# Half-wise turning of the first head's tiles, and two of four mask pieces marked on ScalarE: an attention layer with layer norm on one Trainium2 core

## The reference

```
N, HID, H = 2048, 256, 8             # x (2048, 256), adj (2048, 2048); n = 2048 tokens, d = 256
q = (x @ Wq).reshape(h, n, d); k = (x @ Wk).reshape(h, n, d); v = (x @ Wv).reshape(h, n, d)
a = einsum('hnd,hmd->hnm', q, k) * d**-0.5 + adj + adj
mask = adj == 0.0                     # about 255 of 256 elements
a = where(mask, -1000000.0, a); a = softmax(a); a = where(mask, 0.0, a)
out = einsum('hnm,hmd->hnd', a, v).transpose(1, 0, 2).reshape(n, h * d) @ Wout
return layernorm(x + out)
```

## Time and profile before

| | us |
|---|---|
| median of 3 runs | 1821.1 (1816.62 to 1823.1) |
| the profiled execution, device time | 1819.0 |
| its span, first to last instruction | 1817.3 |

### The profile page before, as it was taken

How to read it: one execution, slowest core, us unless ns; L and a number is a source line. 1 busy time by engine, 2 the same in 40 slices (tenths; PEclk the granted TensorE clock), 3 DMA queues, 4 the chain that set the end, 5 groups by cost and what they waited for, 6 DMA issues and landing times.

```text
span 1817.3 us, 29365 instructions
## 1 busy us (share of the span) xinstructions
PE 1791.5 (99%) x10272; PEld 1580.1 (87%) x10272; DVE 1097.2 (60%) x2318; ACT 852.5 (47%) x1411; POOL 983.7 (54%) x762
## 2 busy tenths in 40 slices
PE   8999899999999999999999999999999999999998
PEld 7987789888998889988898888988889888998886
DVE  6888855555555655555555555555555555546666
ACT  5654555444544445444454444544454444544433
POOL 7878864444644455455564445644455455544443
PEclk9999999999999999999999999999999999999999
DMA  7888875666646666566665666656665566655664
GB/s 252 252 254 270 265 222 155 197 184 189 190 142 200 193 181 197 143 197 189 189 185 157 199 186 180 184 157 198 197 188 158 165 198 200 183 156 174 183 171 133
DMA packets 186995, 345.97 MB, mean 190 GB/s; under 512 B 39392, under 2 KB 96736, under 8 KB 170464
## 3 DMA queue, kind: packets, MB, share of 16 engines
q10 hardware_dynamic: 92032, 200.59, 35.4%
q1 hardware_dynamic: 94816, 143.50, 28.7%
HBM read 190.84 MB, written 18.87 MB: 115 GB/s over the span
## 4 chain that ended last, share of the span: by engine, by line
PE 85%; SPq 5%; DVE 2%; DMA 2%; issue 1%; ACTq 0%; POOL 0%; ACT 0%; DVEq 0%
PE bank L409 33%; PE y_bank L425 22%; PE bank L374 18%; PE y_bank L433 12%; SPq L313 4%; DMA p_turned<-blocks 2%; DVE blocks L683 1%; ACTq L590 0%; POOL p_split L491 0%; DVE y_acc L770 0%; SPq L292 0%; DVE p_split L776 0%; PE bank L394 0%; ACT p_split L562 0%; DVE y_acc L705 0%
## 5 line engine op out<-in xcount | busy, mean ns | idle before, releaser
L491 POOL TENSOR_TENSOR p_split<-p_turned,p_split 128x512 fp32r<-128x512 f32 x510 | 650.1, 1304 | 543.3 <-ACT p_split L562 542.8
L409 PE MATMUL bank<-k_split,q_split 128*128 128x512 f32 x3072 | 788.2, 392 | 3.9 <-DVE small L660 3.9
L409 PEld LDWEIGHTS bank<-k_split,q_split 128*128 128x128 f32 x3072 | 556.5, 189 | 106.1 <-DVE small L660 5.2
L425 PE MATMUL y_bank<-v_split,p_split 128*128 128x512 f32 x2048 | 546.4, 389 | 1.3 <-ACT p_split L562 1.1
L660 DVE CUSTOM_DVE_ANT_0 t_p<-bank,m_sb 128x512 f32<-128x512 f32 x512 | 351.6, 687 | 212.1 <-PE bank L409 183.7
L425 PEld LDWEIGHTS y_bank<-v_split,p_split 128*128 128x128 f32 x2048 | 383.7, 188 | 83.1 <-ACT p_split L562 2.4
L553 ACT ACTIVATE t_p<-t_p,small 128x2048 f32<-128x2048 f32 x128 | 256.9, 2007 | 359.6 <-DVE small L672 351.0
L480 POOL TENSOR_TENSOR w_slot<-raw_w,w_slot 128x512 fp32r<-128x512 f32 x192 | 250.1, 1304 | 252.0 <-ACT w_slot L533 248.9
L562 ACT ACTIVATE p_split<-p_turned 128x512 fp32r<-128x512 f32 x512 | 288.0, 620 | 109.1 <-DMA p_turned<-blocks 105.4
L683 DVE STREAM_TRANSPOSE blocks<-t_p 128x2048 f32<-128x2048 f32 x128 | 295.9, 2312 | 65.9 <-ACT t_p L553 46.5
L374 PE MATMUL bank<-x_t,w_slot 128*128 128x256 f32 x2304 | 306.3, 285 | 7.7 <-issue 4.9
(11 more groups left out here) (44 smaller groups left out, 619.2 us busy)
## 6 DMA issues: line engine op xcount, KB each, us to landing
m_sb<-m_dram ACTq DMA_DIRECT2D x112, 1024.0 KB, 5.3
p_turned<-blocks SPq DMA_DIRECT2D x1532, 64.0 KB, 2.2
p_turned<-blocks ACTq DMA_DIRECT2D x516, 64.0 KB, 2.9
blocks<-in_adj_dram SPq DMA_DIRECT2D x64, 256.0 KB, 4.2
raw_w<-in_L_gnn_Wv_dram ACTq DMA_DIRECT2D x64, 256.0 KB, 3.4
m_dram<-m_sb SPq DMA_DIRECT2D x16, 1024.0 KB, 6.5
raw_w<-in_L_gnn_Wq_dram ACTq DMA_DIRECT2D x63, 256.0 KB, 3.4
raw_w<-in_L_gnn_Wk_dram ACTq DMA_DIRECT2D x61, 256.0 KB, 3.8
```

What stands on the lines that cost most here:

```text
L409: mm = nc.tensor.matmul(dst[:], q[:, a, k, f * P:(f + 1) * P], k_split[:, kk, k, b * BANK:(b + 1) * BANK], start=(i == 0), stop=(i == len( ...
L425: nc.tensor.matmul(y[:], p_split[tau % 2][:, HI, j * P:(j + 1) * P], v_split[:, j].rearrange("p s d -> p (s d)"), start=(j == 0), stop=False)
L491: nc.gpsimd.tensor_tensor(lo, p_turned[:, i * BANK:(i + 1) * BANK].rearrange("p (j b) -> p j b", b=QUAD), hi.bitcast(F32), ALU.subtract).t ...
```

## The change

1. **Halves.** In the first head (`in_halves`) the turn is two transposes of 128 x 1024, bands j = 0, 1 and then j = 2, 3. Each half waits for the exponential and for the shuffling of the same half of the tile before. The semaphores `shuffled` exist for each quarter and half, `turned` counts two a tile. SyncE issues the first half of all four quarters (8 transfers) after the first transpose, then j = 2 of all four (4 transfers) after the second; ScalarE's j = 3 are as before. The high part of a quarter waits for both halves.
2. **Marks on ScalarE.** For pieces 1 and 2 of tiles 1 to 15 VectorE no longer marks, and ScalarE makes Sign of the adjacency (into int8, 1 where it isn't zero) and, after a wait for that, Relu(-2^100 x sign + 2^100), which is 2^100 at the zeros and 0 elsewhere, with its row sum as the count. Both pieces are done one after the other at b = 1. GpSimd then subtracts this from the adjacency where it added before. VectorE scales the two counts back, and sums the counts at the head of the next iteration (`sum_counts`), where it was done after piece 3.
3. GpSimd fills a column with 2^100 as its first instruction, and ScalarE waits for it before its first weight load.

```
-    def shuffle(tau, i):
+    def shuffle(tau, i, columns):
         if i == 0:
-            sp.wait_ge(turned, tau + 1)
+            sp.wait_ge(turned, 2 * tau + 1 if in_halves(tau) and columns.start == 0 else 2 * tau + 2)
         if tau:
             sp.wait_ge(p_lo, 4 * (tau - 1) + i + 1)
-        for j in range(moved_by_sync(tau)):
+        for j in columns:
             sp.dma_start(p_turned[quad(j), i * BANK:(i + 1) * BANK],
-                         turned_place(tau)[quad(i), j * BANK:(j + 1) * BANK]).then_inc(shuffled[i], 16)
+                         turned_place(tau)[quad(i), j * BANK:(j + 1) * BANK]
+                         ).then_inc(shuffled[i][j // 2], 16)
...
                 load_y(t // 2)
-        for i in range(QUADS):
-            if tau:
-                shuffle(tau - 1, i)
-            if i == 1 and t == LAST_Q and h + 1 < H:
-                load_x(h + 1)
+        if tau and in_halves(tau - 1):
+            for i in range(QUADS):
+                shuffle(tau - 1, i, range(0, 2))
+                if i == 1 and t == LAST_Q and h + 1 < H:
+                    load_x(h + 1)
+            for i in range(QUADS):
+                shuffle(tau - 1, i, range(2, moved_by_sync(tau - 1)))
+        elif tau:
+            for i in range(QUADS):
+                shuffle(tau - 1, i, range(0, moved_by_sync(tau - 1)))
+                if i == 1 and t == LAST_Q and h + 1 < H:
+                    load_x(h + 1)
...
 def _(pool):
+    nc.gpsimd.memset(big[:], BIG).then_inc(big_filled, 1)
...
         pool.wait_ge(m_scaled, by_pool[a])
-        nc.gpsimd.tensor_tensor(m_piece(a), m_piece(a), adj_place[q].rearrange("p (r c) -> p c r", c=C),
-                                ALU.add).then_inc(m_by_pool, 1)
+        adj_piece = adj_place[q].rearrange("p (r c) -> p c r", c=C)
+        if marked_by_act(a):
+            nc.gpsimd.tensor_tensor(m_piece(a), adj_piece, m_piece(a), ALU.subtract).then_inc(m_by_pool, 1)
+        else:
+            nc.gpsimd.tensor_tensor(m_piece(a), m_piece(a), adj_piece, ALU.add).then_inc(m_by_pool, 1)
...
             act.wait_ge(y_done, tau - 1)
-        act.wait_ge(shuffled[i], 64 * (tau + 1))
+        act.wait_ge(shuffled[i][0], 32 * (tau + 1))
+        act.wait_ge(shuffled[i][1], 32 * (tau + 1))
...
             act.wait_ge(max_ready, t - 1)
-        act.wait_ge(marked, a + 1)
+        act.wait_ge(marked, nth_mark[a])
         nc.scalar.activation(m_piece(a), zero_mark[q % 2][:].rearrange("p (r c) -> p c r", c=C), ACT.Copy,
                              scale=-BIG).then_inc(m_scaled, 1)
 
+    def mark_zeros(t, q):
+        a = t * BANKS + q
+        if t >= 2:
+            act.wait_ge(m_stored[t % 2], 16 * (t // 2))
+            act.wait_ge(max_ready, t - 1)
+        act.wait_ge(adj_loaded[q], 16 * (t + 1))
+        if nth_signed[a] > 1:
+            act.wait_ge(m_scaled, by_pool[max(e for e in nth_signed if e < a)])
+            act.wait_ge(counted, t)
+        nc.scalar.activation(signs[:], adj_place[q], ACT.Sign).then_inc(signed, 1)
+        act.wait_ge(signed, nth_signed[a])
+        nc.scalar.activation(m_piece(a), signs[:].bitcast(U8).rearrange("p (r c) -> p c r", c=C), ACT.Relu,
+                             scale=-BIG, bias=big[:],
+                             accum_out=big_count[:, ACT_MARKS.index(q):ACT_MARKS.index(q) + 1]
+                             ).then_inc(m_scaled, 1)
+
     def shuffle(tau, i):
         if i == 0:
-            act.wait_ge(turned, tau + 1)
+            act.wait_ge(turned, 2 * tau + 2)
         if tau:
...
             act.dma_start(p_turned[quad(j), i * BANK:(i + 1) * BANK],
-                          turned_place(tau)[quad(i), j * BANK:(j + 1) * BANK]).then_inc(shuffled[i], 16)
+                          turned_place(tau)[quad(i), j * BANK:(j + 1) * BANK]
+                          ).then_inc(shuffled[i][j // 2], 16)
...
                 hi_p(tau - 2, 2 * b + 1)
-            if tau + 1 < TILES and b:
+            if tau + 1 < TILES and b == 1:
+                for q in ACT_MARKS:
+                    mark_zeros(t + 1, q)
+            if tau + 1 < TILES and b and b not in ACT_MARKS:
...
     def turn(tau):
-        if tau and turned_before(tau) is not None:
-            for i in range(QUADS):
-                dve.wait_ge(shuffled[i], 64 * (turned_before(tau) + 1))
-        elif tau:
+        if tau and turned_before(tau) is None:
             dve.wait_ge(m_by_pool, len(by_pool))
             dve.wait_ge(m_by_dve, len(by_dve))
-        dve.wait_ge(exp_done, tau + 1)
-        nc.vector.transpose(turned_place(tau)[:].rearrange("p (q j b) -> p j q b", q=QUADS, b=QUAD),
-                            t_p[:].rearrange("p (j q b) -> p j q b", q=QUADS, b=QUAD)
-                            ).then_inc(turned, 1)
+        for part in range(2) if in_halves(tau) else (None,):
+            if tau and turned_before(tau) is not None:
+                for i in range(QUADS):
+                    for half in (part,) if part is not None else range(2):
+                        dve.wait_ge(shuffled[i][half], 32 * (turned_before(tau) + 1))
+            dve.wait_ge(exp_done, tau + 1)
+            q = slice(0, QUADS) if part is None else slice(2 * part, 2 * part + 2)
+            nc.vector.transpose(
+                turned_place(tau)[:].rearrange("p (q j b) -> p j q b", q=QUADS, b=QUAD)[:, :, q],
+                t_p[:].rearrange("p (j q b) -> p j q b", q=QUADS, b=QUAD)[:, :, q]
+                ).then_inc(turned, 2 if part is None else 1)
...
 
+    def sum_counts(t):
+        if t:
+            dve.wait_ge(m_scaled, by_pool[t * BANKS + ACT_MARKS[-1]])
+            nc.vector.tensor_scalar(chunk_count[:, ACT_MARKS[0]:ACT_MARKS[-1] + 1], big_count[:],
+                                    1.0 / BIG, None, ALU.mult).then_inc(unscaled, 1)
+            dve.wait_ge(unscaled, t)
+        dve.wait_ge(marked, max(n for e, n in nth_mark.items() if e // BANKS == t))
+        nc.vector.tensor_reduce(count[:, t:t + 1], chunk_count, AX_X, ALU.add).then_inc(counted, 1)
+        dve.wait_ge(counted, t + 1)
+        nc.vector.tensor_scalar(no_mask[:, t:t + 1], count[:, t:t + 1], 0.0, NO_FLOOR,
+                                ALU.is_equal, ALU.mult).then_inc(floor_part, 1)
+        dve.wait_ge(floor_part, t + 1)
+        nc.vector.tensor_scalar(maxima[:, t, BANKS:BANKS + 1], no_mask[:, t:t + 1], FLOOR, None,
+                                ALU.add).then_inc(floors, 1)
+
     def build(t, q):
         a = t * BANKS + q
+        if marked_by_act(a):
+            return
...
                 dve.wait_ge(m_stored[t % 2], 16 * (t // 2))
-            dve.wait_ge(marked, a + 1)
+            dve.wait_ge(marked, nth_mark[a])
             nc.vector.scalar_tensor_tensor(
...
                 op0=ALU.mult, op1=ALU.add).then_inc(m_by_dve, 1)
-        if q == BANKS - 1:
-            dve.wait_ge(marked, a + 1)
-            nc.vector.tensor_reduce(count[:, t:t + 1], chunk_count, AX_X, ALU.add).then_inc(counted, 1)
-            dve.wait_ge(counted, t + 1)
-            nc.vector.tensor_scalar(no_mask[:, t:t + 1], count[:, t:t + 1], 0.0, NO_FLOOR,
-                                    ALU.is_equal, ALU.mult).then_inc(floor_part, 1)
-            dve.wait_ge(floor_part, t + 1)
-            nc.vector.tensor_scalar(maxima[:, t, BANKS:BANKS + 1], no_mask[:, t:t + 1], FLOOR, None,
-                                    ALU.add).then_inc(floors, 1)
+        if a == BANKS - 1:
+            sum_counts(t)
...
                 moments((tau - LAG - 1) % TILES)
+        if 1 <= tau < TILES:
+            sum_counts(tau)
         if tau + 1 < TILES:
             build(t + 1, 0)
         if 1 <= tau < ALL:
```

24 lines of the change are left out of this document (20 added, 4 removed).

## The result

| | before | after |
|---|---|---|
| median, 14 runs each on one chip, us | 1819.83 (1816.62 to 1823.41) | 1823.1 (1820.45 to 1826.31) |
| profiled execution, device time | 1819.0 | 1826.3 |
| its span | 1817.3 | 1824.6 |
| ScalarE busy | 852.5 | 878.1 |
| VectorE busy | 1097.2 | 1093.7 |

The ratio of after to before is 1.0017, 95% interval 1.0009 to 1.0024: the change costs about 3 us. That is within the 0.3% that counts as the same, but on the other side of the forecast (6.4 us faster), and it lies 0.1 us above the end of the range. The profiled execution of after is the highest of its 14. The same kernel, profiled again as e11, has a span of 1820.5 us, 3.2 above before, and is the nearer look where the size of the loss counts.

The account below looks back on a forecast made before the run. First head bound by the turn-transfer-landing loop, 13.0 us a tile, later heads by TensorE. To 12.1 + 0.3 = 12.4: 6.6 us over eleven steps, less 0.2 at the start, 1821.1 - 6.4 = 1814.7 us; range 1808.5 to 1823.

Parts of the forecast that it names:

- The queue turns into one without idle: 12.1 us a tile: SyncE's queue, first head: starting transfers sooner removes 0.9 us idle a tile, 13.0 to 12.1, with the same number of transfers.
- The prediction's loop: First head, tiles 3 to 14: VectorE's turn, SyncE's twelve transfers, landing, next turn; 13.0 us a tile, forecast 12.4.
- nothing is won: Rival, chance 0.20: transfer engines are the limit, a shorter queue only lengthens landings, second half-turn still waits; 1820 us.
- the 0.3 us for later landings: First-head transfers: landings 0.6 us later allowed, counted as 0.3 us a tile over the two kinds of tile.
- They need all pieces, so this costs little: ScalarE's high parts: they start after the exponential anyway, and the last piece lands as late as before; little cost.
- The scaling of the two counts comes in, 0.16 us: VectorE, each tile: one small added instruction, priced like the reduction over four numbers, 0.16 us.
- Start: 0.2 us: ScalarE's first weight load waits for GpSimd's fill, delaying TensorE's first projection; 0 to 0.4 us, 0.2 taken.
- Relu with its sum: ScalarE's marks: Relu reading a bias column and writing a row sum, taken at 0.87 us a piece.
- half a turn: VectorE, first head: one 128x1024 transpose, taken at 1.2 us, letting the first eight transfers start sooner.
- that rival: Table switches on ScalarE, chance 0.04: Sign outside the exponential's set, two table loads a tile; 17 us more, 1838 us.
- slower through ScalarE: Rival, chance 0.12: ScalarE's lump of marks waits for adjacency loads; at 13.6 us a tile, 1828 us.
- the ceiling of 10.4: TensorE's stops from 160 to 250 us: 9.5 us idle plus 7 x 0.135 hidden, the most the change can return.

Follow-up runs that it names:

- e11: The changed kernel (after) unaltered, profiled and measured again beside e12; ratio to before 1.0014, span 1820.5 us.
- the light kernels: Kernels storing and reading back only the first 512 of 2048 columns of each mask tile; ratios to before 0.9943 to 0.9960.
- e1: After with halved turn and transfers only; all marks back on VectorE, no fill at the start; ratio to before 1.0011.
- e12: After with the two counts scaled by two one-number instructions, the repeat run of e3; ratio to before 1.0010.
- e5: As e1, but SyncE issues its twelve transfers in the old order, quarter by quarter, after both half turns; ratio to before 1.0001.
- e2: After with turn and transfers undivided, so only the marks on ScalarE remain; ratio to before 1.0035.
- e9: Before with four small VectorE probe multiplications a tile from the third head on (1, 2, 3 numbers, 2 apart); one run, no ratio given.
- e4: After with turn and transfers undivided and the two counts scaled by one-number instructions; ratio to before 1.0007.
- e14: After undivided, ScalarE's marks only from tile 4 on, both counts scaled in one instruction; ratio to before 0.9997.
- e8: After undivided, ScalarE's marks only from tile 4 on, the two counts scaled one by one; ratio to before 0.9998.
- e6: Before with only the first 512 of 2048 columns of each mask tile stored and read back; ratio to before 0.9954.
- e16: The kernel of e6 (before with the light mask store) run again; ratio to before 0.9951.
- e7: e1 with only the first 512 of 2048 columns of each mask tile stored and read back; ratio to before 0.9943.
- e3: After with the two counts scaled by two one-number instructions instead of one instruction on both; ratio to before 1.0029.
- e13: e1 with halves only up to tile 10, turn and transfers undivided from tile 11 on; ratio to before 1.0001.

## Why the prediction was wrong

**"The queue turns into one without idle: 12.1 us a tile."** This is the step that failed. The idle time did go (8.1 to 2.9 us), and the first transfers start earlier. But the step took the length of the twelve issues as fixed, and that is not so: they took 8.0 us in the light kernels, 8.66 in before, 9.5 in after. That is 0.85 us more a tile, 7.7 in the nine tiles from 85 to 204 us, and 4.7 of it are the waits for GpSimd's low parts shown above. The chain that ended last passes there, after:

```profile
186.16 3.04 DMA p_turned<-blocks
...
189.31 0.64 ACT p_split L594
...
190.02 5.06 POOL p_split L519 x4
195.07 0.10 SPq L332
```

Before's chain goes from the landing to the next turn and back to SyncE's issues. This one goes from the landing over ScalarE's high part and GpSimd's four low parts to SyncE's issues, which wait for them, and the chains of e1, e11 and e12 do so too. The prediction's loop didn't have this way. It is not the only limit, though, since e5 has hardly any of these waits and a pace of 13.03. The pace stayed at 12.9 to 13.1 in every kernel with the full traffic, whichever engine had been relieved, and went to 12.1 to 12.4 in every kernel without the store's three quarters. The prediction's rival "nothing is won", at 0.20, has the outcome and half of the mechanism: the landings did get longer, but the second half of the turn waited for one in one tile of twelve in after (two in e1). In the sum, the 0.3 us for later landings is the mis-sized term: what was needed was 0.9 to 1.0.

**"They need all pieces, so this costs little."** This failed too, and what the waits show as cost of the halves comes from it: the late high parts, and the late low parts behind them. The premise was that the last piece lands as late as before. With all of j = 2 issued at the end, though, all four quarters become whole together and late, where they had become whole one after the other. ScalarE, which works in order, then waits: 2.3 us before, 7.1 with the old order (e5), 16.4 with the new (e1), 19.9 in after (where the marks add to it, see e2 and e4). After's TensorE in order of time, 202 to 210 us:

```profile
202.04 1.64 PE L436 MATMUL bank<-k_split,q_split 128*128 128x512 f32 x6
206.09 1.83 PE L452 MATMUL y_bank<-v_split,p_split 128*128 128x512 f32 x4 [2.41 <-ACT p_split L594]
207.72 2.58 PE L436 MATMUL bank<-k_split,q_split 128*128 128x512 f32 x6
```

What is queued behind the wait suffers too. ScalarE from 226 to 240 us, after:

```profile
228.41 0.62 ACT L564 ACTIVATE w_slot<-raw_w 128x512 fp32r<-128x512 f32 x1
...
233.64 0.63 ACT L594 ACTIVATE p_split<-p_turned 128x512 fp32r<-128x512 f32 x1 [4.61 <-DMA p_turned<-blocks]
...
235.17 0.62 ACT L564 ACTIVATE w_slot<-raw_w 128x512 fp32r<-128x512 f32 x1
```

The next head's weight (235.17) stands behind the high parts, and TensorE's chain of waits there has a hole:

```profile
234.43 3.73 issue
238.16 1.83 PE bank L401 x7
```

The prediction listed who waits for the exponential and left out who stands behind a late quarter.

**What the profiled runs lost, in sum.** The stretch from 205 to 250 us in e11, in e1, and in e9, whose first head is before's:

```profile
205.00:250.00 45.00, 39.26 (x226) 34.25 (x227) 32.03 (x69) 28.63 (x52) 34.38 (x27) 0.96 0.87 267
```
```profile
205.00:250.00 45.00, 42.14 (x238) 37.24 (x237) 31.67 (x76) 26.96 (x46) 35.69 (x27) 0.92 0.89 271
```
```profile
205.00:250.00 45.00, 39.83 (x231) 35.07 (x232) 31.17 (x73) 26.40 (x46) 33.40 (x25) 0.96 0.88 276
```

The second head's first scores come 8.2 us later in after than in before. TensorE's idle from 160 to 250 us accounts for 11.0 - 9.5 = 1.5, tile 3's later scores for 2.2, and the granted clock of 0.89 for 0.11 x 45 = 5.0 us of work at full speed: 8.7. For e11 it is -0.1, 2.0 and 0.04 x 45 = 1.8, together 3.7 of 4.2. For e1 the idle is 8.15, so -1.4, with 0.1 before 160 us; the start gives -0.5 and the clock 3.6: together 1.8 of 1.9. So in these executions TensorE's idle time was hardly longer than before, in e1 even shorter, and the lower clock behind the stops made up the rest. This is a term that the prediction doesn't have at all. It can't simply be charged to the change: e9, with the first head of before, has 0.96 there too, and its second head starts at 243.9 us where it starts at 241.6 in before's profile. Against e9, e11 is 1.9 us late at the second head and was 2.0 late at tile 3 already, and e1 is 0.4 early. So before's profile is a lucky one in this respect, and the part of the loss that stands in both comparisons is the late start of tile 3, 2 of about 3 us.

**"The scaling of the two counts comes in, 0.16 us."** Mis-sized by nine: 1.43 us. The form with more than one number in a partition waits for GpSimd's running instruction (e9). In the undivided kernel from tile 1 on it costs 5 us (e2 against e4), from tile 4 on nothing (e14), with halves nothing measurable (e12 against e11). The prediction priced it by a row of a reduction over four numbers, which doesn't wait. A rule of the Trainium skill spoke against that price and was not weighed: "SBUF — State Buffer", section "Who interferes with whom", says that a tensor_scalar whose operands meet the conditions can enter a mode that takes the port pair shared with GpSimd, that whichever comes second blocks for the whole instruction, and that a reduction never contends on this chip. The probes on two numbers agree, 90 of 90.

**"Start: 0.2 us."** The fill was what was looked at. What costs is the lump of marks: four ScalarE instructions and two sum reads stand in tile 0 ahead of the key's weights. ScalarE, 24 to 28 us, after:

```profile
24.49 0.63 ACT L625 ACTIVATE signs<-blocks 128x512 int8<-128x512 f32 x1
25.15 0.78 ACT L627 ACTIVATE m_sb<-signs,big 128x512 f32<-128x512 uint8 x1
...
26.41 0.62 ACT L564 ACTIVATE w_slot<-raw_w 128x512 fp32r<-128x512 f32 x1
```

and TensorE's stop behind them:

```profile
28.48 1.66 PE L401 MATMUL bank<-x_t,w_slot 128*128 128x256 f32 x12 [0.97 <-issue]
```

A second new stop, of 0.99 us, ends at 62.25 us, for VectorE (1.16 in e11). Tile 3 is 2.2 us late (2.0 in e11), and with no gain in the loop behind it that delay is never made up. Kernels that leave the first tiles alone (e8, e14) have neither the delay nor a loss.

**What came out as said.** Sign 0.63 us (0.65 taken), Relu with its sum 0.765 + 0.188 (0.87), half a turn 1.24 (1.2), no function table loaded between the two, so that rival is out. The adjacency made ScalarE wait 1.0 us in nine tiles (3.8 in e11), so "slower through ScalarE" by that mechanism is out too (e4, with 8.3 us of such waits, was 1.0007). The later heads were untouched. TensorE's stops in the head's last tiles are where a changed pace shows: in the light kernels nearly all but those for the next head's weights went, and the run was 8 to 9 us shorter undivided (e6, e16) and 10.3 in e7 (two runs), under the ceiling of 10.4.

**What stays open.** Differences under 0.1% between these kernels are not separable: e1's loss, after against e3 and e12. That the parts don't add up (marks alone 1.0035, halves alone 1.0011, both 1.0014 to 1.0017) has no tested cause. How the halved pace divides between the busy transfers and the way over the low parts wasn't separated either. Whether the store's bytes or its place in the queue set the pace is open. None of the kernels with the whole computation beats before; e8 and e14 equal it.

## What to carry to other kernels

Before a queue's idle time is counted as a gain, look at how busy the transfer engines are in that stretch, and leave some traffic out once as a test: at 0.85 to 0.9 the idle came back as longer issues, later landings and waits for free places. When a transfer is cut in parts and reordered, follow the last part instead of the first: who waits for it, what stands behind that one in its engine's order, and whether the way leads back to the queue. An instruction of VectorE that handles a few numbers isn't cheap by size: with two or more numbers in a partition this one waited for GpSimd, with one it never did, so two instructions were cheaper than one. And one profile is a thin base for a difference of 2 us: the same first head, profiled twice, ended 2.3 us apart.

## What the runs showed of the hardware

- A `tensor_scalar` of two fp32 numbers in each partition takes 0.16 us beside an idle GpSimd, 1.43 on the mean in after from 85 to 204 us and 3.3 at most in its run, and ends when GpSimd's running instruction ends (90 of 90 in e9, 14 of 15 in after). With one number it took 0.15 in all 96 cases of e9.
- Twelve issues of 64 KB transfers by SyncE took 8.0, 8.66 and 9.5 us, by how busy the transfers were and in which order they were issued, waits for free places among them.
- After a stop TensorE can go on at the lower clock. The six matmuls at 207.72 above take 2.58 us, the six ahead of the stop 1.64. The 4 us behind the stop, after, by stretches:

```profile
206.00:210.00 4.00, 3.91 (x10) 2.85 (x11) 3.84 (x12) 3.05 (x7) 4.00 (x4) 0.57 1.06 360
```

The granted clock is 0.57 in it, so most of it is at 1.2 GHz of 2.4. Such a stretch begins at a stop or within 1.5 us behind it also in e1 (from 205.7 us, stop of 2.1), e13 (from 178.1, stop of 2.2) and e8 (from 206.9, stop of 1.45), and in the first head of 13 of the 18 traces in all. The length of the stop doesn't decide: behind the 2.58 us stop of before there is none, behind the same stop in e9 (2.61) there is one, and e12 has none behind stops of up to 2.8.
